# Queries split into high and low parts on 128 partitions, and stacked by DMAs within SBUF

## The reference, cut to what matters

```python
x = x + 0.5 * ffn(layernorm(x))      # 8 experts, the best 2 of each row, 128 -> 512 -> 128, gelu
x = x + attention(layernorm(x))
x = x + 0.5 * ffn(layernorm(x))

def attention(x):                    # 16 heads of 64; one key and one value head for all of them
    q = (x @ Wq) * 64 ** -0.5
    k, v = split(x @ Wkv)
    sim = q @ k.T + bias(rel_emb) * 8            # causal
    return softmax(sim) @ v @ Wout + bout
```

## Time and profile before

| | |
|---|---|
| median of 3 runs | 1218.73 us (1217.48 to 1219.61) |
| the profiled execution, its own time | 1218.79 us |
| its span in the profile | 1217.1 us |
| PE busy | 977.7 us, 80% of the span |
| DVE busy | 748.1 us, 61% |
| ACT busy | 639.3 us, 53% |
| POOL busy | 627.0 us, 52% |

### The profile page before, as it was taken

The page is one execution under the profiler, slowest core; times in us unless marked ns, Lnnn a source line. Parts: engine busy times, 40 slices in busy tenths (PEclk is TensorE's granted clock), DMA queues, the critical chain, the costliest instruction groups (busy, mean ns, idle before and its releaser), DMA issues.

```text
span 1217.1 us, 23933 instructions
## 1 busy us (share of the span) xinstructions
PE 977.7 (80%) x7212; PEld 821.4 (67%) x7212; DVE 748.1 (61%) x2441; ACT 639.3 (53%) x1671; POOL 627.0 (52%) x457
## 2 busy tenths in 40 slices
PE   1516999918888999999999999999996238888870
PEld 1516999916666777777777777877775237777760
DVE  4682222249898888888788888786874662222226
ACT  1201333318778888888888888887873002222220
POOL 2144444367777444535445454454541147777773
PEclk9996999958999999999999999999997569999995
DMA  6888788710010000000000000000002025555546
GB/s 194 129 98 267 209 208 209 178 47 25 25 27 23 1 2 2 1 2 1 1 2 2 1 2 2 2 1 2 1 2 70 0 58 153 152 153 154 148 105 207
DMA packets 66825, 87.14 MB, mean 72 GB/s; under 512 B 8802, under 2 KB 38500, under 8 KB 66704
## 3 DMA queue, kind: packets, MB, share of 16 engines
q1 hardware_dynamic: 57344, 66.60, 20.2%
q0 software_dynamic: 9360, 19.03, 7.2%
HBM read 65.15 MB, written 20.97 MB: 71 GB/s over the span
## 4 chain that ended last, share of the span: by engine, by line
PE 65%; DVE 12%; DMA 9%; issue 5%; POOL 4%; ACT 3%; another core or an unknown queue 0%; DVEq 0%; SPq 0%; POOLq 0%; ACTq 0%
PE bank L1171 12%; PE bank L1155 11%; PE bank L1148 8%; PE bank L1098 7%; PE bank L1108 7%; PE bank L1149 6%; DMA xr<-xn_dram,gidx 5%; PE bank L1178 5%; DVE in_tile L856 2%; PE bank L1055 2%; PE bank L1034 2%; POOL y_dram L587 2%; PE bank L1035 1%; PE bank L1036 1%; PE bank L1090 1%
## 5 line engine op out<-in xcount | busy, mean ns | idle before, releaser
L633 POOL TENSOR_TENSOR prob<-prob,rsum 128x512 f32<-128x512 f32 (+3 forms) x128 | 296.0, 2321 | 267.4 <-DVE rsum L999 267.3
L701 ACT ACTIVATE prob<-prob,negmax 128x384 f32<-128x384 f32 (+3 forms) x512 | 282.9, 554 | 57.2 <-DVE negmax L992 53.9
L992 DVE CUSTOM_DVE_ANT_0 prob<-bank,bias_tab 128x384 f32<-128x384 f32 (+3 forms) x512 | 237.6, 486 | 68.0 <-PE bank L1149 61.3
L675 ACT ACTIVATE hT<-bank 128x512 f32<-128x512 f32 x144 | 86.0, 597 | 328.2 <-PE bank L1098 328.2
L1148 PE MATMUL bank<-kst,qst 128*128 128x256 f32 (+2 forms) x512 | 192.2, 385 | 12.9 <-DVE negmax L992 10.0
L581 POOL DMA_INDIRECT xr<-xn_dram,gidx x144 | 138.0, 958 | 118.6 <-PE bank L1090 67.9
L1155 PE MATMUL bank<-ident,prob 128*128 128x128 f32 x1280 | 190.0, 275 | 0.0
L924 DVE COPY yo<-bank 128x128 f32<-128x128 f32 x144 | 42.1, 292 | 210.7 <-PE bank L1108 195.0
L1171 PE MATMUL bank<-pT,vst 128*64 128x256 f32 x1280 | 166.4, 389 | 4.9 <-DVE pT L1005 3.1
L1155 PEld LDWEIGHTS bank<-ident,prob 128*128 128x128 f32 x1280 | 152.4, 141 | 25.6 <-issue 11.4
L1149 PE MATMUL bank<-kst,qst 128*128 128x256 f32 (+2 forms) x512 | 162.9, 327 | 0.0
(11 more groups left out here) (153 smaller groups left out, 1252.6 us busy)
## 6 DMA issues: line engine op xcount, KB each, us to landing
w1t<-L_ffn_fc_w SPq DMA_DIRECT2D x144, 256.0 KB
bias_dram<-hg SPq DMA_DIRECT2D x1, 5120.0 KB, 52.9
y_dram<-yo SPq DMA_DIRECT2D x72, 64.0 KB
xn_dram<-in_tile SPq DMA_DIRECT2D x8, 512.0 KB, 3.0
bias_tab<-bias_dram SPq DMA_DIRECT2D x1, 4096.0 KB, 13.1
in_tile<-y_dram SPq DMA_DIRECT2D x8, 512.0 KB, 4.4
xr<-xn_dram,gidx POOLq DMA_INDIRECT x144
x_sb<-L_attn_x SPq DMA_DIRECT2D x4, 512.0 KB, 9.3
```

Of the source, the lines that this page charges most:

```text
L633: g.tensor_tensor(out=pv, in0=pv, in1=rsum[:, n % 8, :].unsqueeze(2).to_broadcast([P, HG, (n % QT + 1) * P]), op=ALU.mult).then_inc(norm_d ...
L701: a.activation(prob[n % 8][:, h, :], prob[n % 8][:, h, :], ACT.Exp, scale=-1.0, bias=negmax[:, i % 8:i % 8 + 1], accum_out=lsum[:, n % 8, ...
L992: v.tensor_tensor_reduce(out=prob[n % 8][:, h, :], in0=BANK_OF["S", b, n, h][:, 0:w], in1=bias_tab[:, HG * (n // QT) + h, SEQ - w:SEQ], sc ...
```

## The change

QH becomes one activation over 128 partitions into a new tile `qhl` (plane 0), QL one instruction over 128 partitions into plane 1 of it. Four DMAs of SP, each of 64 partitions x 2048 bytes, then copy the four quarters (head o, part z) to where they were before in `qst`. `qhl` is a single tile, so a QH waits until the DMAs of the pair before have landed (the semaphore `q_in`, 64 for each pair). The scores wait for the same semaphore in place of `misc_free`. In the planner's table QH costs 0.5 instead of 0.98, QL 0.62 instead of 1.1, QH needs the QL of the pair before, and whatever needs a QL is put 3.0 us after it (`landing`); so the order on all engines is worked out anew.

```diff
+            qhl = ab("qhl", [P, 2, SEQ], F32R)
...
-                        task(("QH", b, g, c), {"act": 0.98}, [("Q", b, g, c)] + [("S", b2, g2 * QT + QT - 1, h) for h in (2 * c, 2 * c + 1)])
-                        task(("QL", b, g, c), {"dve": 1.1}, [("QH", b, g, c)], None, ("Q", b, g, c))
+                        task(("QH", b, g, c), {"act": 0.5}, [("Q", b, g, c), ("QL", b, g, c - 1) if c else ("QL", b, g - 1, 1) if g else ("QL", b - 1, NG - 1, 1)] + [("S", b2, g2 * QT + QT - 1, h) for h in (2 * c, 2 * c + 1)])
+                        task(("QL", b, g, c), {"dve": 0.62}, [("QH", b, g, c)], None, ("Q", b, g, c))
...
-                            hop = HOP["landing" if k[0] == "GA" else "same" if other == e else "pe" if e == "pe" else "other"]
+                            hop = HOP["landing" if k[0] in ("GA", "QL") else "same" if other == e else "pe" if e == "pe" else "other"]
...
+            def restack_sp():
+
+                for i, k in enumerate(RESTACKED):
+                    _, b, g, c = k
+                    sp.wait_ge(misc_free, MISC_FREE[k])
+                    b2, g2 = (b, g - 2) if g >= 2 else (b - 1, g - 2 + NG)
+                    if b2 >= 0:
+                        sp.wait_ge(s_ps, max(S_PS["S", b2, g2 * QT + QT - 1, h] for h in (2 * c, 2 * c + 1)))
+                    for o in range(2):
+                        for z in range(2):
+                            sp.dma_start(qst[z * DH:(z + 1) * DH, g % 2, 2 * c + o, :].bitcast(F32), qhl[o * DH:(o + 1) * DH, z, :].bitcast(F32)).then_inc(q_in, 16)
...
-                        for o in range(2):
-                            a.activation(qst[0:DH, g % 2, 2 * c + o, :], BANK_OF["Q", b, g, c][DH * o:DH * o + DH, :], ACT.Copy,
-                                         scale=DH ** -0.5).then_inc(misc_hi, 1)
+                        if Q_IN["QL", b, g, c] > 64:
+                            act.wait_ge(q_in, Q_IN["QL", b, g, c] - 64)
+                        a.activation(qhl[:, 0, :], BANK_OF["Q", b, g, c][:], ACT.Copy, scale=DH ** -0.5).then_inc(misc_hi, 1)
...
-                        for o in range(2):
-                            dve.wait_ge(misc_hi, MISC_HI["QH", b, g, c] - 1 + o)
-                            ins = v.scalar_tensor_tensor(out=qst[DH:P, g % 2, 2 * c + o, :], in0=BANK_OF["Q", b, g, c][DH * o:DH * o + DH, :],
-                                                         scalar=DH ** -0.5, in1=qst[0:DH, g % 2, 2 * c + o, :].bitcast(F32),
-                                                         op0=ALU.mult, op1=ALU.subtract)
-                        ins.then_inc(misc_free, 1)
+                        dve.wait_ge(misc_hi, MISC_HI["QH", b, g, c])
+                        v.scalar_tensor_tensor(out=qhl[:, 1, :], in0=BANK_OF["Q", b, g, c][:], scalar=DH ** -0.5, in1=qhl[:, 0, :].bitcast(F32),
+                                               op0=ALU.mult, op1=ALU.subtract).then_inc(misc_free, 1)
...
-                            pe.wait_ge(misc_free, MISC_FREE["QL", b, g, h // 2])
+                            pe.wait_ge(q_in, Q_IN["QL", b, g, h // 2])
```

More of the change, by code:

```diff
@@ L205, in build @@
         out_done = sem("out_done")
+        q_in = sem("q_in")
         comb1, combined = sem("comb1"), sem("combined")
@@ L407, in build @@
         AV_PS, PROJ_PS = counted("pe", ("AV",)), counted("pe", ("Y",))
-        MISC_HI = counted("act", ("xTh", "KH", "QH"), lambda k: 2 if k[0] == "QH" else 1)
+        MISC_HI = counted("act", ("xTh", "KH", "QH"))
         V_DONE, EXP_DONE, OT_DONE = counted("act", ("VC",)), counted("act", ("EXP",)), counted("act", ("O",))
@@ L412, in build @@
         XA_DONE, PROJ_DONE = counted("dve", ("LN",), QT), counted("dve", ("YA",))
+        RESTACKED = [k for k in ORDER["dve"] if k[0] == "QL"]
+        Q_IN = {k: 64 * (i + 1) for i, k in enumerate(RESTACKED)}
         NORM, BOUT = counted("pool", ("N",)), counted("pool", ("BO",))
@@ L442, in build @@
                     in_order(("S", b2, g2 * QT + QT - 1, h), k)
+        for first, second in zip(RESTACKED, RESTACKED[1:]):
+            in_order(("QH", *first[1:]), ("QH", *second[1:]))
         for k in ORDER["dve"]:
@@ L507, in ffn_sp @@
                     sp.dma_start(yc[:, gi - 4, :, :], yd[:, 4 * gi:4 * gi + 4, :]).then_inc(y2_in[gi - 4], 16)
+            def restack_sp():
[8 more added lines that the diff above has]
+                            sp.dma_start(qst[z * DH:(z + 1) * DH, g % 2, 2 * c + o, :].bitcast(F32), qhl[o * DH:(o + 1) * DH, z, :].bitcast(F32)).then_inc(q_in, 16)
             ffn_sp(0)
+            restack_sp()
             ffn_sp(1)
```

## The result

The changed kernel takes 1277.45 us (median of 4 runs, 1275.99 to 1282.51), the kernel before 1218.11 us beside it. The ratio is 1.0494, with a 95% interval of 1.0462 to 1.0526. Forecast were 1238 us and a range of 1212 to 1264: the direction was right, the size was not. The execution that was profiled took 1282.51 us, the longest of the four.

A forecast was written before the change was run, and what follows sets the result against it. PE was taken to bound the kernel, with its waits paid in full. Landing waits of +22 us (groups 2, 3) and +3 us (group 1), less 6 us relief, gave +19 on 1218.79: 1238 us, range 1212 to 1264.

The forecast's parts named there:

- 3.6 us at most: Attention from 440 to 900 us: PE busy 456.40 of 460 us, so faster DVE or ACT could win only this.
- two groups out of 16: Groups of kinds 2 and 3 lying where PE idles anyway; left out, so 14 were counted at 1.54 us each, 22 us.
- The relief: DVE and ACT time saved by one QH and one QL per pair, mostly beside PE's work: 6 us gain, bounds 0 and 13.
- L: Time from the end of a QL to the landing of its four DMAs: 1.4 fixed + 4 x 0.60 = 3.8 us.
- the count of landings that are paid: Attention groups whose waits cost: 14 of kinds 2 and 3 at 1.54 us, 7 of kind 1 at 0.4, none of group 0.
- hidden up to 3.4, 0.4 late at 3.8: Group 1: PE has 5.7 us from second Q to S of head 2, 2.35 + L needed; 3 us over 7 groups.
- the chain: Q to S of head 2 in groups 2 and 3: 3.75 + 2L against 9.81 us of PE work, 1.54 us late.
- these two overlap: Groups 2 and 3: Y 1.3 us late behind ACT's O, S of head 2 1.54 us late; only 1.54 counts.
- the forecast's own 3.3 to 4.4: Range of L, in us, belonging to the forecast: 1221 to 1258 us, chance 0.50.
- rival B: L 4.4 or more, as small copies queue with part of their fixed cost: +46 us at 4.6, 1265 us; chance 0.18.
- What I said would show it: PE idle 1 to 2 us per group 2 and 3, about 96% busy from 440 us, early stretch some 5 us shorter.
- One of my signs of being wrong: Idle time of PE in all four groups, which would mean L above 4.2 us.

The follow-up runs named there:

- e13_wide: The kernel before with its own order, only QH and QL over 128 partitions, no copies or stacking: 1210.43 us, ratio 0.9931.
- e2_nostack: The changed kernel's order and QH and QL over 128 partitions, without the copies, their waits or the stacking: 1210.01 us, ratio 0.9932.
- e9_traffic: `e2_nostack` plus as many narrow copies of the same size, into a tile nobody reads, that only SP waits for: 1211.44 us, ratio 0.9936.
- e8_table2: The changed kernel, one place of qhl, with 4.8 us for a QL's landing in the planner's table and Q due earlier (4.5): 1216.55 us, ratio 0.9995.
- e7_all: The changed kernel with two places of qhl, 5.0 us in the table, Q due 4.0 ahead, one rule on Q dropped: 1205.66 us, ratio 0.9894.

## Why the prediction was wrong

**What bounds the kernel** held: it is PE, and PE's waits are paid. Two bounds that I read from busy shares did not hold. One was that from 440 to 900 us a faster ACT or DVE could win 3.6 us at most. `e13_wide`, in the order of before, has this there:

```profile
440.00:900.00 460.00, 456.76 (x3324) 360.20 (x3324) 339.39 (x1245) 359.63 (x1060) 228.00 (x101) 1.00 0.01 1
```

PE is busy as long as before (456.40), with 52 matmuls more. At the last Y of batch 1, near 461 us, this kernel is 0.4 us ahead of the one before, at the last Y of attention 6.9 us: a share of 99% did not mean that PE ran at its peak. The other was that waits up to 400 us partly fall into idle time, so that I left two groups out of 16. `e2_nostack` ends batch 0 at 374.9 us and the changed kernel, with the same lists, at 382.1: the waits of batch 0 cost 7 us, nearly as much as those of any later batch (53 us in the last six).

**The relief** was 6 us forecast and 8 measured (`e2_nostack`, `e13_wide`). Where it falls depends on the order: `e2_nostack` has 6.4 us of it by the end of batch 0, as I had read it, and `e13_wide` none by then.

**The step that failed first is L**, "L = 1.4 + 4 x 0.60 = 3.8 us". Measured are 4.28 us for an undisturbed landing, and 4.35 at the median of those waited for. Both terms were short. The fixed part is 1.15 us up to the first data and 0.45 from the last to the waiting engine, 1.6 for my 1.4; the data of the four take 3.84 - 1.15 = 2.7 us for my 2.4. The transfer rate was about right: the packets of 2048 bytes took 137 ns on average, so 16 engines move 16 x 2048 / 0.137 = 239 GB/s, near the 219 that I took from the earlier trace rows, and the four would need 2.2 us by it. The nearness is partly luck: I took the flow from 10 to 12 us for that of the two narrow loads, but two wide loads of x, issued at 2.41 and 3.09 us, landed only at 15.2 and 16.5. What was wrong is what bounds the four. I had the issues at 0.33 to 0.5 us, from DMAs of other shapes, and let the transfers set the pace. A copy of 64 partitions takes SP 0.60 us, and with the gap behind it 0.64, more than the 0.55 of its transfer, so the last one begins at 1.81. Four wide copies land only 0.25 us sooner. The Trainium skill's rule on the ports ("SBUF — State Buffer", section "Door 1") is borne out in the packets: 137 ns for 2048 bytes on 64 partitions against 85 ns in the two wide copies. The rule is right and was given too much weight: the width is 0.25 of the 4.28 us.

**The step that failed second is the count of landings that are paid.** What failed is that group 1 is "hidden up to 3.4, 0.4 late at 3.8" and group 0 "hidden". Beside `e2_nostack`, the time from a group's first Q to its S of head 2 is longer by 2.2, 2.8, 2.8 and 2.6 us in groups 0, 1, 2 and 3 (means of batches 2 to 7), where the sum at 4.28 has 0, 0.9, 2.5 and 2.5. For groups 2 and 3 the chain holds: it says 3.75 + 8.56 - 9.81 = 2.5 us, and the group shown has 1.03 of idle PE before its Y and 1.15 before its S, 2.2. I had said that these two overlap and the larger counts; the chain's total has both, one behind the other, and is right as a total. For groups 0 and 1 I looked only at each group's own two landings. With a single tile, the first QH of a group can also wait for the last landing of the group before, and pushes EXP and O back on ACT: 16 of the 32 QH that waited, and 12 of the 32 S, are of groups 0 and 1.

**The third is a term that the sum did not have: the clock.** The granted clock stood longer at its lower level than in `e2_nostack` (0.89 instead of 0.93 from 271 to 400 us, 0.99 instead of 1.00 from 440 to 900), and that cost 7.5 us in the changed kernel (table above). `e9_traffic`, with copies and without the waits, has 1.00 in the later stretch, so there the clock fell with the waits; in the early one it has 0.90, so there that is not shown.

With an L of 4.5 (the mean with the late ones: last data at 4.07 on average, and 0.45 until the landing is seen), my sum gives 14 x 2.94 + 7 x 1.1 - 6 = +43 us, 24 more than forecast. Its waits are then 49 us, and 60.7 were measured: 12 more from the count. The clock and the rest of the table add 9, and the relief was 2 larger. That makes 43 of the 44 us by which the profiled execution lay above the forecast; its time is 5 us above the median.

No case of the forecast was the one that came. The undisturbed L of 4.28 lies inside the forecast's own 3.3 to 4.4, the mean of 4.5 in rival B, and B had +46 us at 4.6 where +59 were measured at less; its cause, a fixed cost that does not overlap, was not the one either.

**What I said would show it** did in part: idle time ended by the landing or by ACT's O, before a Y or an S. The share of PE went down to 92% where I had 96, and the early stretch was not 5 us shorter: batch 0 ended 0.8 us later than before. One of my signs of being wrong came too, idle time in all four groups, which I had tied to an L above 4.2.

## What to carry to other kernels

In this kernel a row of small copies landed 2.2 to 2.6 us after the last of them was issued (four narrow, four wide and two wide ones). So price such a row as (number of copies - 1) x issue time of that very shape, plus one whole landing, as long as a transfer is about as short as an issue, and try fewer copies before wider ones. A single tile between a producer and a copy ties each landing to the next, also across groups that look covered by themselves. Where an order is worked out from a table, look at the table first: a landing that it had 1.3 us too short lost 67 us beside the kernel without copies, and that one number gave back 52. With the first step of the chain due early enough as well, the kernel was as fast as before (`e8_table2`), and with a second tile faster (`e7_all`). And a busy share of 99% was no bound on what could be won.

## What was not expected of the hardware

About a quarter of the landings are late: in 17 of the 64 sets of copies the last data came over 4.2 us after QL. In the changed kernel a packet of 16 KB of instruction code, which sits on one DMA engine for about 1 us, overlapped the data of 12 of the sets. Their last data came 4.80 us after QL at the median, that of the other 52 sets at 3.84. One such stretch, 562 to 564.5 us:

```profile
q1 hardware_dynamic: 181, 0.28, 47.9%
q8 instruction: 1, 0.02, 2.7%
```

```profile
559.69 2.38 SPq L525 DMA_DIRECT2D qst<-qhl  x4
...
565.31 0.36 PE L1164 MATMUL bank<-kst,qst 128*128 128x256 f32 x1 [1.68 <-DMA qst<-qhl]
```

Its copies were issued from 559.69 us on without delay, and landed 5.6 us later. No run took the code packets away, so this is a coincidence in time, seen 12 times, and not shown as the cause. Ten of the 256 issues on SP also took 0.9 to 1.8 us instead of 0.6. The tables that did best held 4.8 and 5.0 us, with other changes beside it, so what a margin for the late landings is worth was not measured apart.
